# Two attentions of a decoder kernel: value products in two passes, their halves joined by three engines

## The reference

```python
# first: 16 heads of 32
att = q @ k.T * 32**-0.5 + causal_mask;  w = softmax(att)
x = x + (w @ v).reshape(B, T, D) @ Wo.T
# second: 32 query heads of 64 in 8 groups, one key and one value head per group, q and k rotated
qk = where(causal, rope(q) @ rope(k).T * 64**-0.5, -inf);  attn = softmax(qk)
x = x + concat(attn @ v) @ w_out.T
```

## Time and profile before

| | us |
|---|---|
| median of 3 runs | 1911.99 (1911.48 to 1913.77) |
| the profiled execution | 1911.71 |
| its span in the profile | 1910.3 |
| mean granted clock of TensorE | 0.984 of full speed |
| TensorE busy | 1805.9 |
| VectorE, ScalarE, GpSimd busy | 1116.6, 805.1, 1007.6 |

### The profile page before, as it was taken

One profiled execution on the slowest core, in us unless ns is written; L12 is line 12 of the kernel. 1 busy time (PEld: TensorE's weight loads), 2 busy tenths in 40 slices (PEclk: granted clock), 3 DMA queues, 4 the chain that ended last, 5 costly groups with the idle time before them and its releaser, 6 DMA issues. The chain is left out here.

```text
span 1910.3 us, 30804 instructions
## 1 busy us (share of the span) xinstructions
PE 1805.9 (95%) x10161; PEld 1568.9 (82%) x10167; DVE 1116.6 (58%) x2769; ACT 805.1 (42%) x2063; POOL 1007.6 (53%) x965
## 2 busy tenths in 40 slices
PE   7999989999999999999879999999999999999996
PEld 5888857788999999899668988888888888867796
DVE  6676885663333333336756666666666757565345
ACT  3767643222222222221366666565565433543232
POOL 3444342387874867895456455455453203116783
PEclk8999999999999999999999999999999999999999
DMA  3556430246663645554343234233321210012666
GB/s 113 162 166 205 144 138 1 81 157 224 230 209 124 214 153 176 183 153 121 90 111 100 62 95 105 67 88 91 79 71 56 74 50 1 24 50 67 222 215 199
DMA packets 104551, 232.54 MB, mean 122 GB/s; under 512 B 20672, under 2 KB 20928, under 8 KB 101328
## 3 DMA queue, kind: packets, MB, share of 16 engines
q1 hardware_dynamic: 84080, 144.31, 24.8%
q0 software_dynamic: 19744, 85.47, 13.5%
q10 hardware_dynamic: 576, 0.79, 0.2%
HBM read 126.23 MB, written 57.93 MB: 96 GB/s over the span
## 5 line engine op out<-in xcount | busy, mean ns | idle before, releaser
L706 POOL TENSOR_SCALAR a_E<-a_E,a_inv 128x128 f32<-128x128 f32 (+3 forms) x384 | 221.0, 593 | 224.2 <-DVE a_inv L842 224.2
L739 ACT ACTIVATE a_E<-a_E,a_top 128x512 f32<-128x512 f32 (+3 forms) x384 | 211.1, 567 | 5.1 <-DVE a_top L836 5.0
L153 PE MATMUL bank<-f_UH,f_XH 128*128 x596 | 200.7, 337 | 8.0 <-issue 3.4
L153 PE MATMUL bank<-f_UH,f_XL 128*128 x596 | 193.4, 324 | 0.0
L153 PE MATMUL bank<-f_UL,f_XH 128*128 x596 | 193.4, 324 | 0.0
L731 ACT ACTIVATE a_PHL<-bank 128x512 fp32r<-128x512 f32 (+1 forms) x288 | 130.8, 528 | 133.2 <-PE bank L1025 133.2
L836 DVE CUSTOM_DVE_ANT_0 a_E<-a_causal,bank 128x512 f32<-128x512 bf16 (+3 forms) x384 | 163.7, 481 | 29.3 <-PE bank L1009 17.6
L153 PE MATMUL bank<-a_PHL,a_VH 128*128 128x512 f32 (+3 forms) x768 | 180.5, 324 | 0.3 <-DVE a_QL L165 0.3
L165 DVE TENSOR_TENSOR a_PHL<-bank,a_PHL 128x512 fp32r<-128x512 f32 (+1 forms) x288 | 153.7, 587 | 9.7 <-ACT a_PHL L731 9.5
L1807 ACT ACTIVATE f_HH<-bank 128x256 fp32r<-128x256 f32 x220 | 59.8, 323 | 232.2 <-PE bank L2204 232.1
L1862 DVE TENSOR_TENSOR f_gate<-bank,f_gate 128x352 f32<-128x352 f32 x79 | 41.3, 523 | 191.7 <-PE bank L153 191.6
(11 more groups left out here) (407 smaller groups left out, 4875.7 us busy)
## 6 DMA issues: line engine op xcount, KB each, us to landing
f_uraw<-f_up POOLq DMA_DIRECT2D x18, 1408.0 KB, 6.5
f_xb<-table SPq DMA_DIRECT2D x86, 256.0 KB, 3.4
table<-f_ob SPq DMA_DIRECT2D x86, 256.0 KB, 2.7
table<-a_zeros SPq DMA_DIRECT2D x31, 512.0 KB, 3.9
f_draw<-f_down POOLq DMA_DIRECT2D x27, 512.0 KB, 4.5
a_g<-a_f SPq DMA_DIRECT2D x160, 64.0 KB, 2.0
a_raw<-a_qkv SPq DMA_DIRECT2D x36, 256.0 KB
f_uraw<-f_up POOLq DMA_DIRECT2D x9, 704.0 KB, 4.5
```

What stands on the lines that cost most here:

```text
L153: m = pe.matmul(out, a, b, start=first and i == 0 and j == 0, stop=last and i == n - 1 and j == 2, skip_group_check=not check)
L706: e.tensor_scalar(self.E[sl][:, a], self.E[sl][:, a], self.inv[:, sl, i:i + 1], 0.0, ALU.mult, ALU.add).then_inc(*self.s_nrm.up(N, m - 1, i))
L739: x = e.activation(E, E, ACT.Exp, scale=-1.0, bias=self.top[:, sl, i:i + 1], accum_out=self.total[:, sl, i:i + 1])
```

## The change

- `VH` and `VL` become one tile `V`: a head's high values stand in its columns, its low values in the columns of the other half (64 further on, modulo 128). Values are two matmuls per block, `V` with `PH` and `V` with `PL`. A half of 64 rows of the bank then holds the high part's sum and the other half the low part's. (The product of the two low parts is now included.)
- So the bank is opened and closed for each half of 64 rows: every two heads in the first attention, every head in the second. ScalarE copies the half's own rows to `QH` and the other rows to `S`; VectorE writes the low part of the own rows to `R`, in the next loop after the reciprocal; when both halves of a tile are there, GpSimd adds `R` and `S` into `QL`, one loop after ScalarE, ahead of the normalization. Output products wait for that addition.
- Output products stand a loop later in `FILL`, and value projections of the second attention sooner; `SPLIT` follows.
- Values are staged in a tile of their own, `W`, not in a slot.
- In the second attention the rotated low part of loop m-1's projection is made at the end of VectorE's loop m, not after the reciprocal of loop m+1, and its transfers follow the turn's of loop m on SyncE's queue.
- GpSimd clears one value tile in place of two in the first attention and none in the second.

```diff
-        self.VH, self.VL = sb("VH", [heads, NT, P], F32R), sb("VL", [heads, NT, P], F32R)
+        self.V = sb("V", [heads, NT, P], F32R)
+        self.S, self.R, self.W = sb("S", [T]), sb("R", [T]), sb("W", [T])
...
-            self.FILL = [[("P", K, 1), ("O", 2, -1), ("O", 3, -1)], [("P", 0, 1)], [("P", V, 1)],
-                         [("O", 4, -1), ("O", 5, -1), ("T", 1)],
-                         [("P", K, 0, 1), ("O", 6, -1), ("O", 7, -1)], [("P", 0, 0, 1)], [("P", V, 0, 1)],
-                         [("O", 0), ("O", 1), ("T", 0, 1)]]
+            self.FILL = [[("P", K, 1), ("O", 0, -1), ("O", 1, -1)], [("P", 0, 1), ("O", 2, -1), ("O", 3, -1)],
+                         [("P", V, 1)], [("T", 1)], [("P", K, 0, 1), ("O", 4, -1), ("O", 5, -1)],
...
-            self.FILL = [[("P", 1, 0)], [("P", 2, 0)], [("P", K, 1)], [("O", 4, -1), ("O", 5, -1)],
-                         [("P", 3, 1)], [("O", 6, -1), ("O", 7, -1)], [("P", V, 1)], [("T", 1), ("P", 0, 1)],
-                         [("P", 1, 1)], [("P", 2, 1)], [("P", K, 0, 1)], [("O", 0), ("O", 1)], [("P", 3, 0, 1)],
-                         [("O", 2), ("O", 3)], [("P", V, 0, 1)], [("T", 0, 1), ("P", 0, 0, 1)]]
-            self.SPLIT = {4: (K, 1), 5: (self.wt, 0), 6: (self.wt + 1, 0), 7: (self.wt + 2, 0), 8: (self.wt + 3, 0),
-                          9: (3, 1), 10: (V, 1), 11: (0, 1), 12: (1, 1), 13: (2, 1)}
+            self.FILL = [[("P", 1, 0)], [("P", 2, 0)], [("P", K, 1)], [("P", V, 1)], [("O", 4, -1), ("O", 5, -1)],
+                         [("P", 3, 1)], [("O", 6, -1), ("O", 7, -1)], [("T", 1), ("P", 0, 1)],
+                         [("P", 1, 1)], [("P", 2, 1)], [("P", K, 0, 1)], [("P", V, 0, 1)], [("O", 0), ("O", 1)],
+                         [("P", 3, 0, 1)], [("O", 2), ("O", 3)], [("T", 0, 1), ("P", 0, 0, 1)]]
+            self.SPLIT = {4: (K, 1), 5: (V, 1), 6: (3, 1), 7: (self.wt, 0), 8: (self.wt + 1, 0), 9: (self.wt + 2, 0),
+                          10: (self.wt + 3, 0), 11: (0, 1), 12: (1, 1), 13: (2, 1)}
...
+                        self.staged[j, b], self.free[x[1:]] = self.W[:, :], turned
+                        turned = [self.s_vt.after(N, j, b)]
+                        continue
-                    if c == self.vt:
-                        self.staged[j, b] = self.f[s].bitcast(F32)
-                        freed[s] = [self.s_vt.after(N, j, b)]
-                        continue
...
+    def low_columns(self, cs):
+
+        at = (cs.start + self.HALF) % P
+        return slice(at, at + self.hd)
+
+    def halves(self, h):
+
+        own = slice(self.half(h) * self.HALF, (self.half(h) + 1) * self.HALF)
+        return own, slice((1 - self.half(h)) * self.HALF, (2 - self.half(h)) * self.HALF)
...
-            for x in self.projected(m - 2 if self.rotary is not None else m):
-                e.wait_ge(*self.s_lo.after(N, *x))
-                self._move(e, x, 0)
-                if x not in self.shared_moves:
-                    self._move(e, x, 1)
+            if self.rotary is None or m < 1:
+                self._moves(m if self.rotary is None else m - 2)
             if self.rotary is not None:
                 for x in self.projected(m):
                     self._turn(x)
+                if m >= 0:
+                    self._moves(m - 1)
             elif 2 <= m < 2 + len(self.k.clearings):
                 if m == 2:
...
-        for z in (self.VH, self.VL):
-            e.memset(z[:, :, :, :].bitcast(F32), 0.0)
+        if 2 * self.hd < P:
+            e.memset(self.V[:, :, :, :].bitcast(F32), 0.0)
...
+            if 4 <= m < self.M + 4 and self.jobs[m - 4][3] == self.heads - 1:
+                j, b, r, h = self.jobs[m - 4]
+                e.wait_ge(*self.s_olo.after(N, j, r, b, self.half(h)))
+                e.tensor_tensor(self.QL[:, r, b * T:b * T + T], self.R[:, :], self.S[:, :], ALU.add).then_inc(
+                    *self.s_rest.up(N, j, r, b))
             if 1 <= m <= self.M:
                 sl = (m - 1) % self.SLOTS
...
-            if 3 <= m < self.M + 3 and self.jobs[m - 3][3] == self.heads - 1:
+            if 3 <= m < self.M + 3 and self.closes(self.jobs[m - 3][3]):
                 j, b, r, h = self.jobs[m - 3]
+                own, other = self.halves(h)
+                bank = self.k.bank[self.OB]
                 e.wait_ge(*self.s_av.after(N, m - 3))
-                e.activation(self.QH[:, r, b * T:b * T + T], self.k.bank[self.OB][:, :], ACT.Copy).then_inc(
-                    *self.s_ohi.up(N, j, r, b))
+                if m - 3 >= self.heads:
+                    e.wait_ge(*self.s_rest.after(N, *self.pair(m - 3 - self.heads)))
+                e.activation(self.QH[own, r, b * T:b * T + T], bank[own, :], ACT.Copy)
+                e.activation(self.S[own, :], bank[other, :], ACT.Copy).then_inc(
+                    *self.s_ohi.up(N, j, r, b, self.half(h)))
 
...
                 e.reciprocal(self.inv[:, sl, :], self.total[:, sl, :]).then_inc(*self.s_inv.up(N, m - 1))
+            if 4 <= m < self.M + 4 and self.closes(self.jobs[m - 4][3]):
+                self._dve_low_values(m - 4)
             if self.rotary is not None:
-                for x in self.projected(m - 2):
-                    s = self.slot[x]
-                    e.wait_ge(*self.s_rhi.after(N, *x))
-                    low_part(e, self.f[s], self.f[s].bitcast(F32), self.g[s],
-                             scale=self.scale if x[1] < self.qtiles else None).then_inc(*self.s_lo.up(N, *x))
+                if m < 1:
+                    self._dve_low_rotated(m - 2)
                 for x in self.projected(m - 1):
                     self._dve_rotate(x)
...
-            if 3 <= m < self.M + 3 and self.jobs[m - 3][3] == self.heads - 1:
-                j, b, r, h = self.jobs[m - 3]
-                a = slice(b * T, b * T + T)
-                e.wait_ge(*self.s_ohi.after(N, j, r, b))
-                low_part(e, self.QL[:, r, a], self.k.bank[self.OB][:, :], self.QH[:, r, a]).then_inc(
-                    *self.s_olo.up(N, j, r, b))
+            if self.rotary is not None and m >= 0:
+                self._dve_low_rotated(m - 1)
+
+    def _dve_low_values(self, m):
+
+
+        e, N, (j, b, r, h) = self.k.dve, self.name, self.jobs[m]
+        (own, other), a, key = self.halves(h), slice(b * T, b * T + T), (N, j, r, b, self.half(h))
+        bank = self.k.bank[self.OB]
+        e.wait_ge(*self.s_ohi.after(*key))
+        if m >= self.heads:
+            e.wait_ge(*self.s_rest.after(N, *self.pair(m - self.heads)))
+        low_part(e, self.R[own, :], bank[own, :], self.QH[own, r, a]).then_inc(*self.s_olo.up(*key))
 
     def _stats(self, loaded, tiles):
...
-                    i = low_part(e, self.VL[:, h, bs, cs], src[:, :, cs], self.VH[:, h, bs, cs], scale=1.0)
+                    i = low_part(e, self.V[:, h, bs, self.low_columns(cs)], src[:, :, cs], self.V[:, h, bs, cs], scale=1.0)
...
-                    e.wait_ge(*self.s_olo.after(N, j, self.queries[-1], g // TT))
+                    e.wait_ge(*self.s_rest.after(N, j, self.queries[-1], g // TT))
...
-        if h == 0 and self.OB in emptied:
+        if self.opens(h) and self.OB in emptied:
             e.wait_ge(*emptied[self.OB])
         for ci, chunk in enumerate(self.TCHUNKS):
             e.wait_ge(*self.s_plo.after(N, m, ci))
             for sblk, _ in chunk:
                 a = slice(self.P_AT[sblk], self.P_AT[sblk] + T - sblk * P)
-                t = product(e, self.k.bank[self.OB][:, sblk * P:T],
-                            [(self.VH[:, h, b * TT + sblk, :], self.VL[:, h, b * TT + sblk, :])],
-                            [(self.PH[m % 2][:, a], self.PL[m % 2][:, a])],
-                            first=h == 0 and sblk == 0, last=h == self.heads - 1 and ci == 2)
+                for x, weights in enumerate((self.PH, self.PL)):
+                    t = e.matmul(self.k.bank[self.OB][:, sblk * P:T], self.V[:, h, b * TT + sblk, :], weights[m % 2][:, a],
+                                 start=self.opens(h) and sblk == 0 and x == 0, stop=self.closes(h) and ci == 2 and x == 1)
         t.then_inc(*self.s_av.up(N, m))
-        if h == self.heads - 1:
-            emptied[self.OB] = self.s_olo.after(N, j, r, b)
+        if self.closes(h):
+            emptied[self.OB] = self.s_olo.after(N, j, r, b, self.half(h))
 
     def projections_done(self):
 
```

More of the change, by code:

```diff
@@ L527, in plan @@
             sig, ("lo", "vlo", "mx", "inv", "plo", "x", "olo", "p1", "p3"))
+        self.s_rest = sig("u")
         self.s_zero, self.s_wlo, self.s_p2, self.s_nrm = map(sig, ("zero", "wlo", "p2", "nrm"))
@@ L545, in plan @@
         self.slot, self.free, self.fill_bank, self.score_bank = {}, {}, {}, {}
-        freed, ring, self.staged = [[], []], 0, {}
+        freed, turned, ring, self.staged = [[], []], [], 0, {}
         for m in self.loops:
@@ L648, in sp, with _moves @@
                     self.k.fetch_context()
+    def _moves(self, m):
+        e = self.k.sp
+        for x in self.projected(m):
```

(11 more changed lines are left out.)

19 lines of the change are left out of this document (16 added, 3 removed).

## The result

The changed kernel takes 1916.93 us (median of 12 runs), the kernel before 1912.45 (12 runs): ratio 1.0024, 95% interval 1.0013 to 1.0036. It is slower by 4.5 us where 6 less were forecast; the time lies inside the range of the prediction, on the other side of no change. The profiled execution took 1917.09, its span is 1915.8, the mean granted clock 0.976 (before 0.984).

What follows compares the result with a forecast made beforehand. TensorE, busy 1805.9 of 1910.3 us, plus short waits was taken as the bound. Terms -60.5 + 14.2 + 38.0 + 6 + 3.8 + 3 - 10.3 gave -5.8, so 1905.9 us; range 1866 to 1932.

Steps and rivals of the forecast that it cites:

- Part 1: Both attentions: values in two matmul passes instead of three save 0.63 us of TensorE per job, -60.5 us.
- Rival D: Values matmuls are paced by weight loads, so two passes save 37 us instead of 60.5; about 1918 us, chance 0.03.
- Part 2, runs: Second attention, behind four rotated projections in a row: the rotation chain slips, 6.0 us of waits per run, +38.0 us.
- own case: The forecast's terms as summed, 1905.9 us; 1895 to 1917 with a run at 4.9 to 7.1 us, chance 0.50.
- Rivals A: Rotation in the runs does not slip; joining costs only the first attention's bank waits and the ends; 1858 us, chance 0.12.
- Rival B: The rotation chain slips but the addition lies off it; 3.4 us a run, 1882 us, chance 0.13.
- C: Same rotation chain, slower: addition 1.79 us, 9.3 a run; kernel slower from 7.6 a run; 1930 us, chance 0.22.
- signs of being wrong: Three: run loops last 6.4 us; transposes wait for VectorE's low parts or output bank; clock falls in over ten places.
- Part 2, T loops: First attention, loops transposing values: last transposes late by about 1.85 us seven times, 1.2 once; +14.2 us.
- Part 3: Second attention, sooner rotated low parts: seven waits for VectorE's low parts and a query's transfer wait go, -10.3 us.
- Ends: At each attention's end the last output products wait for one more copy and the addition, +3.8 us for both.
- Clock: Some 20 expected waits of about 2 us bring four more slow-clock stretches, +6 us, bounds 0 and 30.

Runs made afterwards that it cites:

- two other executions of the same loops: Changed kernel with tail edits only (1911.96 us, 0.9994), and with first-attention output products 2 and 3 moved only (1912.72 us, 1.0002); both leave these loops untouched.
- Filling the loops: Changed kernel with first-attention output products 2 and 3 moved into four of the eight loops that hold only the values' transposes: 1912.72 us, 1.0002.
- The tail's edit: Changed kernel with the last head's values in a bank of their own and ten dummy matmuls ahead of the last wait: 1911.96 us, 0.9994.
- all moves: Changed kernel: addition behind normalization, value projection between rotated ones, output products beside transposes, tail edits: 1918.22 us, 0.9889; with addition on VectorE 1898.46 us, 0.981.
- rotation behind the normalization: Kernel with all moves, plus GpSimd's rotation multiplication behind its normalization and VectorE's rotation steps behind the transposed weights' low parts: 1921.61 us, 0.9896.

## Why the prediction was wrong

**Part 1** held: 0.61 to 0.65 us a job, a values block of 1.26 us (1210.39 to 1211.65), 1.27 forecast. Rival D is out.

**Part 2, runs, is the step that failed, by its size.** The mechanism is the one forecast (own case, not Rivals A or B): the chain of the rotation slips, the addition gets in ahead of VectorE's sum, and transposes are late at n = 2, 3 and 4. Two terms made up the 6.0 us: 3.4 that Rival B kept without the addition, and 2.6 for the addition. The second measured 2.5 (7.7 less 5.2), at most 3.2. The first measured **5.2, not 3.4**. Six runs of 1.7 to 1.8 are 10.4 us, almost the whole of the 11.2 us between the forecast's -5.8 and the profile's +5.4.

The step in the prediction's own terms was "12.6, 21.6, 29.4" for the ends of GpSimd's products: measured 13.6, 22.5 and 30.3. Without the addition I had them at 12.6, 20.3 and 28.1; measured 13.2, 21.5 and 29.3. Two inputs were short. I carried the first product at 1.32 us, the second row, though 1.79 stood there too and the mean of all 40 before was 1.72; in the runs it takes 1.79, as VectorE's multiplication begins 0.05 us before it. And 7.73 us a projection came from one pair of products, where the run without addition shows 8.1. Together they account for 1.2 of the 1.8 us; the rest of the term isn't broken down.

It put the case just under C's deciding point of 7.6 us a run; the measured 7.7 lies just over it, and the sign with it. The two other executions of the same loops, with 8.2 and 8.4, are on the same side. C's own prices (addition 1.79, 9.3 a run) are not what happened: the addition took 1.29, near the 1.32 taken. (The trace before held a nearer row than the multiplications, a subtraction of 128x512 on GpSimd at 1.28 us.)

**What the transposes wait for** was wrong in name, and the prediction had counted this among its signs of being wrong: VectorE's low parts of the last transposes come first (20.7 us), the normalization only 0.34 behind. Both stand behind the same addition, one through VectorE's sum. With the addition behind the normalization the waits for the low parts fall to 11.8, with it on VectorE to 13.2; those for the output bank rise from 8.6 to 13.6 and 12.1.

**Part 2, T loops**: 4.42 and then 8.22 us, against 3.46 forecast for the first and 7.11 that the next loop takes with the same fill: 2.1 late, 1.85 forecast. Right in size, though not all in its place: half of it stands ahead of the T loop's own values, and only the other half at the transposes behind, where the normalization releases them as forecast. Filling the loops returned half.

**Part 3**: -10.3 forecast. Put back, it cost 4.9 us in the median and 6.0 in the stretch, both near the scatter, and the 2.3 us wait of a query's transfer stayed (3.1 in three). About half a term.

**Ends**: 1.9 forecast for the second attention, 6.4 measured. The copy and the addition were there. Missed were the wait of the last head's values for the one output bank (2.0, released by the low part of the head before) and the clock: it is at half from 1474.4 to 1484.6, so it fell behind the bank wait already, and the last values take 2.58 us where those before took 1.54. The tail's edit removed both and gave back 5.4 in its trace.

**Clock**: +6 forecast, for four more stretches at half clock. From the first scores to the last loop of the second attention there are six of 3.4 us where three were (ten and eight in the two other executions of these loops), and the long one in the tail. Over the whole span the mean fell from 0.984 to 0.976: 0.008 x 1916 = 15 us of full-speed time, part of it idle anyway. What it cost in time was not measured by itself. It is no part of what the experiments gained: with the addition behind, 17 us went at the same 0.976.

**A term left out**, which works the other way: the kernel before lost 2.4 us in each of its runs, 14.7 in six, of which the prediction took back 8.0 (the waits of the earlier trace rows). Against the kernel before, the change costs a run 5.3 us and not 7.7.

The terms do not close to a microsecond: runs +10.4, ends +4.5 and the wait that stayed +2.3, less 6.7 for the term left out, are 10.5 for the second attention alone, while its stretch came out some 8 above the forecast (+3.6, where the prediction's terms for it, with two thirds of the clock's, come to about -5). Scatter of 2 to 4 us a stretch holds the difference, and 3.9 of the profile's +5.4 stand in the mixture, which the change does not touch. That part stays open.

## What to carry to other kernels

Before work goes to the least busy engine, look at what stands behind it in that engine's queue at that moment: GpSimd was 55% busy and still the wrong place, while VectorE, at 60%, did the same addition in 0.73 us for nothing that could be measured (1894.2 us with it, 1896.0 without). A shorter loop is worth only what the slowest chain of the loop allows, so cost that chain from several of its instances, with its longest transfer, before counting savings; and leave one suspected term out on the chip to see which share is its own. Count the losses that the kernel before has at the same place, too: only the difference is the price of the change. The version with all moves and the addition on VectorE, 0.981 of the kernel before, is faster than both the kernel before and the changed one.

The Trainium skill ("GPSIMD Engine Reference", section "4.1 Engine selection") sends an elementwise addition of a tile to VectorE and calls GpSimd about 2 times slower for two inputs. The trace agrees: 1291 ns against 730. Moving it was worth 22.8 us of the kernel's time, of which 17 came already with the addition still on GpSimd, behind the normalization.

## What was not expected of the hardware

- GpSimd's addition makes VectorE's sum beside it 1.68 us instead of 0.79, while GpSimd's normalization does not (0.79). VectorE's multiplication, started 0.05 us before GpSimd's, goes with 1.78 us for that one; where GpSimd's starts first, it takes 1.28 to 1.32 and VectorE's 1.65 to 1.78 (and rotation behind the normalization at 1113.88).
- The granted clock in the tail was 0.78, and fell behind a wait of 2.0 us; with that wait gone and ten dummy matmuls in the one of 3.5 us behind it, it was 1.00.
- The kernel before took 1913 us in three batches and 1932 and 1939 in two, one of them on the chip of an earlier batch with 1913.
